# A gated transformer block on one core: e4m3 rounding done on float32 words read as int32, decoded by ScalarE's copies

## What is computed

```python
def _fp8(x):
    return x.astype(jnp.float8_e4m3fn).astype(jnp.float32)

def _reorder_quantize_x(x, idx):
    scale = jnp.max(jnp.abs(x)) / GLOBAL_DIV
    xr = (x / scale)[:, idx]
    scale_x = jnp.max(jnp.abs(xr), axis=1, keepdims=True) / FP8_MAX
    qx = _fp8(xr / scale_x)
    return (qx, scale_x, scale)
...
qx, sx, sc = _reorder_quantize_x(xf, up_reorder_index)
g = _qlinear(qx, sx, sc, w_gate, up_reorder_index, out_idx=down_reorder_index)
u = _qlinear(qx, sx, sc, w_up, up_reorder_index, out_idx=down_reorder_index)
t = jax.nn.silu(g) * u
qt, st, sct = _reorder_quantize_x(t, down_reorder_index)
y = _qlinear(qt, st, sct, w_down, down_reorder_index)
...
x = x + tanh(g_xattn[0]) * xattn(layernorm(x), ctx_512, Wq, Wkv_expand, Wout)
x = x + tanh(g_ffn[0]) * ffn(layernorm(x), w_gate, w_up, w_down, up_reorder_index, down_reorder_index)
```

## Time and profile before

| | |
|---|---|
| time, median of 3 runs | 765.31 us (764.86 to 766.76) |
| span of the profiled execution, first to last instruction | 761.7 us |
| between the span and the median of the runs | 3.6 us |
| busy share: PE, DVE, ACT, POOL | 87%, 92%, 73%, 74% |
| mean granted TensorE clock | 0.967 |

### The profile page before, as it was taken

One profiled execution on the slowest core, in us unless ns is written; L12 is line 12 of the kernel. 1 busy time (PEld: TensorE's weight loads), 2 busy tenths in 40 slices (PEclk: granted clock), 3 DMA queues, 4 the chain that ended last, 5 costly groups with the idle time before them and its releaser, 6 DMA issues.

```text
span 761.7 us, 15793 instructions
## 1 busy us (share of the span) xinstructions
PE 665.4 (87%) x6054; PEld 416.8 (55%) x6130; DVE 701.5 (92%) x1177; ACT 553.4 (73%) x987; POOL 563.7 (74%) x606
## 2 busy tenths in 40 slices
PE   2466888999999999999999999999999999787672
PEld 2455665656565665666665656565656565443220
DVE  6998696999999999999999999999999999997983
ACT  4978888887869696878787878788787857374330
POOL 5588897877878787878787878788787876565351
PEclk9878999999999999999999999999999999999986
DMA  9789775696575657574756584946465655041221
GB/s 290 191 201 187 158 148 102 125 190 122 139 115 133 120 130 133 128 126 107 145 115 131 98 164 83 174 83 167 83 162 102 142 87 124 8 103 26 62 65 46
DMA packets 151209, 95.52 MB, mean 125 GB/s; under 512 B 115327, under 2 KB 121855, under 8 KB 151135
## 3 DMA queue, kind: packets, MB, share of 16 engines
q1 hardware_dynamic: 148974, 92.68, 57.6%
q0 software_dynamic: 576, 1.45, 0.6%
q10 hardware_dynamic: 1584, 0.39, 0.3%
HBM read 31.59 MB, written 9.83 MB: 54 GB/s over the span
## 4 chain that ended last, share of the span: by engine, by line
DVE 54%; ACT 15%; issue 12%; PE 10%; POOL 5%; DMA 2%; ACTq 0%; SPq 0%; DVEq 0%; POOLq 0%; another core or an unknown queue 0%
DVE mx L1687 8%; DVE room L1773 7%; DVE room L1554 6%; DVE mx L1686 5%; PE pair L726 4%; DVE tm L1780 3%; DVE rsum L1691 3%; DVE cx L1735 3%; DVE room L1798 3%; DVE room L1756 3%; ACT PT L1334 2%; DVE room L1558 2%; POOL x L607 2%; POOL PT L587 2%; ACT L1334 2%
## 5 line engine op out<-in xcount | busy, mean ns | idle before, releaser
L603 POOL TENSOR_TENSOR room<-room,up_scale 128x512 f32<-128x512 f32 (+1 forms) x96 | 132.6, 1388 | 42.9 <-ACT room L1359 40.4
L587 POOL TENSOR_SCALAR_AFFINE_SELECT PT<-PT 128x512 f32<-128x512 f32 x128 | 84.5, 678 | 40.5 <-ACT PT L1334 40.2
L1359 ACT ACTIVATE room<-room,sx 128x512 f32<-128x512 f32 (+1 forms) x96 | 65.2, 681 | 57.9 <-DVE room L1756 57.2
L1334 ACT ACTIVATE PT<-pair 128x768 f32<-128x768 f32 x128 | 98.9, 817 | 8.0 <-PE pair L958 7.0
L726 PE MATMUL pair<-WdT,room 128*128 128x512 bf16 x349 | 84.6, 391 | 18.4 <-DMA room<-room 12.8
L726 PE MATMUL pair<-WgT,room 128*128 128x512 bf16 (+1 forms) x370 | 88.4, 361 | 8.1 <-DMA room<-room 4.3
L726 PE MATMUL pair<-WuT,room 128*128 128x512 bf16 (+1 forms) x369 | 89.0, 363 | 2.5 <-DVE room L1756 1.9
L726 PE MATMUL pair<-xT,WqTh 128*128 128x256 bf16 x512 | 87.1, 273 | 1.7 <-ACT exact L1146 1.7
L1364 ACT ACTIVATE room<-room 128x512 bf16<-128x512 f32 (+1 forms) x96 | 54.7, 586 | 45.3 <-DVE room L1773 44.3
L1687 DVE TENSOR_REDUCE mx<-pair 128x2 f32<-128x512 f32 x128 | 86.9, 679 | 0.0
L726 PE MATMUL pair<-xT,WqTl 128*128 128x256 bf16 x256 | 69.8, 272 | 0.0
(11 more groups left out here) (137 smaller groups left out, 1948.7 us busy)
## 6 DMA issues: line engine op xcount, KB each, us to landing
xin<-in_x_dram SPq DMA_DIRECT2D x16, 512.0 KB
K<-kh SPq DMA_DIRECT2D x32, 256.0 KB
Q<-qh SPq DMA_DIRECT2D x32, 256.0 KB
x<-in_x_dram SPq DMA_DIRECT2D x16, 512.0 KB, 4.3
out_dram<-x SPq DMA_DIRECT2D x16, 512.0 KB, 3.1
K<-kl SPq DMA_DIRECT2D x16, 256.0 KB
Q<-kl SPq DMA_DIRECT2D x16, 256.0 KB
room<-in_L_ffn_w_down_dram SPq DMA_DIRECT2D x4, 704.0 KB, 7.4
```

The lines of the kernel that those rows point to most:

```text
L587: pool.affine_select(out=view, in_=view, compare_op=ALU.is_ge, fill=0.0, base=0, pattern=[[0, 2], [0, 2], [1, P]], channel_multiplier=-1). ...
L603: pool.tensor_tensor(g, g, up_scale[:, chunk(n)[1]], ALU.mult).then_inc(slw_done, 1)
L1334: act.activation(head_columns(ring(b, c), 0, 384), head_columns(shifted_pair[c][:, :], 0, 384), ACT.Exp, scale=SCALE).then_inc(exp_done, 1)
L1359: act.activation(g, g, ACT.Silu, scale=sx[:, chunk(n)[0]:chunk(n)[0] + 1]).then_inc(silu_done, 1)
```

## The change

The rounding is done on float32 words. With x * mult * 2^-120 the smallest normal number of e4m3 falls on the smallest normal number of float32, and its step below falls among float32's subnormals. The word, read as int32, is turned to float by VectorE, which adds 1.5 * 2^43 and subtracts it again: that rounds it to a multiple of 2^20, which leaves three fraction bits. The result is written back over the same word. Its upper half is a bfloat16, and a copy by ScalarE with the factor 2^120 decodes it.

- VectorE does `scaled` (factor per row, then 2^-120) and `coded` (on int32) in place of `floored`, `lifted` and `low`: two instructions for a tile and not three, with one input each and 32-bit words in and out.
- ScalarE's absolute values are gone. For x and t a copy takes their place behind `coded` (`taken_x`, `taken_t`), each of a whole tile; for the weights TensorE transposes the upper halves, and the copy that ScalarE made before gets the factor.
- GpSimd no longer rounds weights.
- `q_w` is gone; its room gives six raw slots. Unit u waits for the transposes of unit u - 6 (before: for the rounding of unit u - 4).
- `squares2` of token tile 1 moves ahead of `exps` 6 (`coded` overwrites `cx`), and waits are added for the buffers that are now shared longer.

```diff
-ROUND_FLOOR = 1.5 * 2.0**-6
-ROUND_LIFT = 2.0**20
+CODE = 2.0**-120
+ROUND = 1.5 * 2.0**43
...
-    SLOTS = 4
+    SLOTS = 6
...
+        def code_tile(u, n):
+
+            return raw_tile(u, n).bitcast(BF16).rearrange("p (n two) -> p n two", two=2)[:, :, 1]
...
             def unit_loaded(u):
...
+                if u >= SLOTS:
+                    sp.wait_ge(w_turned, u - SLOTS + 1)
...
             def turn_qt(b, t):
+                if b:
+                    sp.wait_ge(down_made, 2 * b - 1 + t)
                 sp.wait_ge(qt_done, 2 * b + t + 1)
...
-            def abs_t(b, n):
-                act.wait_ge(t_done, 6 * b + n + 1)
-                t, f = chunk(n)
-                act.activation(qt[:, t, f], T[:, t, f], ACT.Abs, scale=ROUND_LIFT).then_inc(abst_done, 1)
+            def taken_t(b, t):
+                act.wait_ge(codedt_done, 2 * b + t + 1)
+                if b:
+                    act.wait_ge(qtT_in[t], 16 * b)
+                act.activation(qt[:, t, :], T[:, t, :], ACT.Copy, scale=1.0 / CODE).then_inc(qt_done, 1)
...
-            def low(dst, w, high):
-                return dve.tensor_tensor(dst, w, high, ALU.subtract)
-
-            def floored(lift, mult):
-
-                return dve.tensor_scalar(lift, lift, mult, ROUND_FLOOR * ROUND_LIFT, ALU.mult, ALU.max)
+            def scaled(w, mult):
+
+                return dve.tensor_scalar(w, w, mult, CODE, ALU.mult, ALU.mult)
+
+            def coded(w):
+
+                return dve.tensor_scalar(w.bitcast(I32), w.bitcast(I32), ROUND, -ROUND, ALU.add, ALU.add)
...
-            def lifted_t(b, t):
-                dve.wait_ge(floort_done, 2 * b + t + 1)
-                dve.scalar_tensor_tensor(out=T[:, t, :], in0=T[:, t, :], scalar=tmult[:, t:t + 1], in1=qt[:, t, :],
-                                         op0=ALU.mult, op1=ALU.add).then_inc(liftedt_done, 1)
-
-            def rounded_t(b, t):
-                dve.wait_ge(liftedt_done, 2 * b + t + 1)
-                low(qt[:, t, :], T[:, t, :], qt[:, t, :]).then_inc(qt_done, 1)
+                scaled(T[:, t, :], tmult[:, t:t + 1]).then_inc(scaledt_done, 1)
+
+            def coded_t(b, t):
+                dve.wait_ge(scaledt_done, 2 * b + t + 1)
+                coded(T[:, t, :]).then_inc(codedt_done, 1)
```

More of the change, by code:

```diff
@@ L15 @@
 BF16 = mybir.dt.bfloat16
+I32 = mybir.dt.int32
 ALU = mybir.AluOpType
@@ L142, in gated_block_kernel @@
         SLOT = max(2 * H, I)
-        room = sb("room", [P, SLOTS * SLOT + SLOTS * SLOT // 2])
+        room = sb("room", [P, SLOTS * SLOT])
         carved = [0]
@@ L228, in raw_tile, with all_tiles @@
             return raw_w[:, u % SLOTS, n * width:(n + 1) * width]
[L230 to L234, removed]
+        def code_tile(u, n):
+            return raw_tile(u, n).bitcast(BF16).rearrange("p (n two) -> p n two", two=2)[:, :, 1]
+        def all_tiles(u):
             j, _, k = UNITS[u]
-            return w[:, u % SLOTS, 0:k * (H if j < 2 else I)]
+            return raw_w[:, u % SLOTS, 0:k * (H if j < 2 else I)]
         def place(head):
@@ L786, in unit_turned @@
                     for m in range(k):
-                        last = pe.transpose(w[:, (i * k + m) * P:(i * k + m + 1) * P], q_tile(u, m)[:, tok(i)], identb[:, :])
+                        last = pe.transpose(w[:, (i * k + m) * P:(i * k + m + 1) * P], code_tile(u, m)[:, tok(i)], identb[:, :])
                 last.then_inc(w_turned, 1)
@@ L998, in gate_products @@
                     pe.wait_ge(qxT_in[1], 16 * b + 16)
+                if n == 3 and b >= 14:
+                    pe.wait_ge(y_done, 2 * b - 1)
                 if n == 3 and b < 14:
@@ L1376, in _ @@
             act.wait_ge(factor_done, 1)
-            for k in range(-8, NB + 1):
+            for k in range(-8, NB + 2):
                 at(k + 3, squares1, 0)
@@ L1678, in unit_rounded, with unit_coded @@
-            def unit_rounded(u):
-                dve.wait_ge(w_lifted, u + 1)
-                low(all_tiles(q_w, u), all_tiles(raw_w, u), all_tiles(q_w, u)).then_inc(w_round_dve, 1)
+                    last = scaled(raw_tile(u, m), wmult[:, j, i + m:i + m + 1])
+                last.then_inc(w_scaled, 1)
+            def unit_coded(u):
+                dve.wait_ge(w_scaled, u + 1)
+                coded(all_tiles(u)).then_inc(w_coded, 1)
             def maxima(b, c):
@@ L1763, in up @@
                     dve.wait_ge(up_made, 6 * b + 3)
+                if n % 3 == 0 and b:
+                    dve.wait_ge(qt_done, 2 * b + n // 3 - 1)
                 if n == 3:
@@ L1934, in _ @@
                 if k == 0:
[L1935 removed]
+                    unit_scaled(14)
                 if k == -5:
[L1937 removed]
+                    unit_coded(2)
                 at(k - 1, gate, 4)
```

382 lines of the change are left out of this document (74 added, 308 removed).

## The result

The changed kernel takes **752.34 us** (median of 4 runs, 750.39 to 752.92) where the kernel before takes 765.25 us beside it (764.86 to 766.76): a ratio of 0.983, 95% interval 0.982 to 0.985. That is 13 us less, and 738 us were forecast, 27 less. A second measurement on another chip gave 749.91 us (748.90 to 754.21), ratio 0.981 (0.978 to 0.985). The first reciprocal came at 95.44 us, so one of the signs of being wrong that the prediction names ("if that reciprocal stays at 96") is met. The profiled execution has a span of 750.5 us and a time of 752.25 us.

What follows compares the result with a forecast made beforehand. DVE was fullest (38.73 us of each 39.90 us period), PE close behind (38.38). Gains of 10.8 (twelve periods), 1.3, 0.5, 0.9, 10 (head) and 4 (end) made 27.5 us: span 734.2, plus 3.6, time 738 us, range 721 to 754.

Steps and rivals of the forecast that it cites:

- if that reciprocal stays at 96: Sign of being wrong: the first reciprocal of softmax sums staying at 96 us, where near 86 us was forecast.
- The instructions (7.0 us a sequence): DVE's new rounding of x and t, waits for GpSimd included: 7.0 us a sequence where it spent 12.4.
- Up to 95.91 ... I take 10: Head, where weights are prepared: DVE and ACT lose work, shortening it by 10 us, between 4 and 18.
- Loads: ... I cost that at nothing: Unit loads with six slots: later ones wait for a transpose on PE, costed at nothing.
- The first periods (2.7): Three periods after the first reciprocal: gains of 1.3 (165.74 to 205.99), 0.5 and 0.9 us.
- The regular period (39.0): Each of twelve periods: 39.0 us, between 38.4 and 40.4, with PE waiting for transposed t before `down` of tile 1.
- as long as ACT reaches the exponentials early: ACT's copy of t's tile 0 between exponentials 3 and 4 (1.4 us): hidden on this condition, otherwise up to 1 us.
- PE takes all: Rival: transposes land in time, periods are PE's 38.4 us, 42.5 us gained, 723 us; chance 0.17.
- `mT` would come 1 us earlier: In each period, DVE's time saved ahead of the third gate brings `mT` 1 us earlier.
- Twelve times 0.9: Twelve periods between 205.99 and 684.81 us, each 0.9 us shorter: 10.8 us.
- The end (4): Last stretch, 684.81 to 761.70 us: 4 us gained, between 0.8 and 9.6.
- the periods don't move: Rival: late landings, late exponentials or slow int32 step; only head, end and first periods gain, 750 us; chance 0.19.

Runs made afterwards that it cites:

- the repeat: The changed kernel itself measured again, nothing edited, on another chip: 749.91 us, ratio 0.981; first reciprocal 93.69 us.
- experiment 7: Changed kernel with the second rounding step (`coded`) on each tile of t done twice: 759.97 us, ratio 0.994 to the kernel before.
- Experiments 2: Changed kernel with the weights' second rounding step (`coded`) done on one column of each unit only: 752.68 us, ratio 0.985 to the kernel before.
- experiment 3: Half the bytes in unit loads from unit 6 on: changed kernel 748.08 us, ratio 0.978; kernel before 763.74 us, ratio 0.9995.
- experiment 11: Changed kernel with only x and t rounded the new way, weights the old way in four slots: 755.39 us, ratio 0.987 to the kernel before.
- experiment 10: Changed kernel with the load of `w_down` issued earlier, ahead of `stack_queries`: 747.82 us, ratio 0.979 to the kernel before.
- experiment 9: Changed kernel with `mT`'s DMA issued by SyncE and not ScalarE: 749.10 us, ratio 0.980 to the kernel before.
- experiment 8: Changed kernel with ScalarE's copy of t's tile 1 moved ahead of taking and sending `mT`: 750.92 us, ratio 0.983 to the kernel before.

## Why the prediction was off, step by step

- **The instructions (7.0 us a sequence)**: held, 6.54. The int32 step runs at the rate that I took; its median on 1408 columns is 894 ns (0.88 forecast), on 512 it is 428 (0.42). DVE is busy 33.9 us in a regular period (33.4 forecast).
- **"Up to 95.91 ... I take 10"** is the step that failed: 0.5 us in the profile, 2.2 in the repeat, 3.3 at most (experiment 7). I added up the time that DVE and ACT lose and looked only for how much of it was on the chain, not for what would be on the chain without it. DVE and ACT had hidden a chain of stacks (keys to `kl`, to K, to `kl` again, to Q, to `mT`, to Q) that is paced by DMAs of 5 to 8.5 us each, and two of these cost TensorE and GpSimd some 3 us more than before (K's low part and `mT`), in traffic that had moved against them. Experiments 2 and 3 show it from both sides: 12 us less on DVE gives nothing, half the bytes give 3 to 4 us, and in the kernel before the same half gives nothing. What ACT's share of the loss was worth by itself, and what the traffic beside `mT` costs, no run shows. My own row with DMA share for the head had it, and I did not read it. Of my bounds, 4 to 18, the lower one was too high: it counted ACT's instructions on the chain as if nothing stood beside them.
- **"Loads: ... I cost that at nothing"** holds as far as it was tried: the early loads crowd the queue (experiment 3), but the kernel with the old four slots (11) is no faster. That run has the old rounding of the weights too, so it does not price the slots by themselves.
- **The first periods (2.7)**: -2.5. Three us of that go with the load of `w_down`, itself late by 1.4 us and in front of the transposed x (experiment 10 gives them back): the work around it moved, the load was issued 2.0 us later, and the transpose followed it by 3.3 us and not by 4.6. It was a transfer that I had not followed at all, since it isn't in the diff. In the second period (37.44 for 36.65) TensorE waits 0.43 and 0.56 us for the exponentials, which it did not before; they stand behind the new copy on ACT.
- **The regular period (39.0)**: 39.05, right, and for the wrong reason, so this hit is luck. I took it as TensorE's 38.4 plus a wait for the transposed t. There is no such wait. The 38.4 is a mean over twelve periods, the last of which has less work for TensorE (33.4 us of busy time before, where the others have 38.9); a regular one after has 38.70. The other 0.35 us are the wait for `PT`, behind the copy of t's tile 0: I had that copy hidden, "as long as ACT reaches the exponentials early", and it is not quite. With my rival "PE takes all" I had set the floor at 38.4; experiment 9 shows 39.05. No run moves the copy of tile 0, so whether the 0.35 us can be had back is open. That `mT` would come 1 us earlier held (19.4 us after the reciprocal and not 20.4), and the path through ACT's copy of tile 1 has 0.4 us of slack (experiment 7).
- **Twelve times 0.9**: 6.7 and not 10.8. The regular ones give 0.8 each (39.87 to 39.06). Three us are lost to two landings of 5.0 us in place of 3.1, half a us to the last. The spread of 3.1 to 5.1 stood in the earlier trace rows; I took the median for all, and with 0.4 us of slack a late landing costs all but these 0.4. The rows mix both tiles: tile 1's alone landed in 4.3 us in most periods, beside `mT`'s DMA, and my reason for the 3.1, that this DMA is no longer on its way then, held.
- **The end (4)**: 6.6, and 5.0 in the repeat: under-sized by 1 to 3 us, and well under the upper bound of 9.6.
- The 3.6 us around the span are 1.8 when the profiled execution's own time is taken. The miss of 14.3 us is 9.5 + 5.2 + 4.1 - 2.6 less these 1.9, to rounding. That the time lies near my rival of 750 us, "the periods don't move", is chance: the regular periods moved by 0.8 us, and it was the head that did not.

## What to carry to other kernels

When work is taken off an engine, the gain ends at the next chain under it: take the engine away in thought and walk the chain again, DMAs and shared buffers included, before adding up what it saves. A DMA's landing isn't one number: with little slack nearly all of a late one is paid, so either give the path slack (here 1 us, from moving one DMA issue off the engine that also makes the data) or count the late ones; and look at what makes them late, since an earlier issue can also take the transfer out of its way. A mean over periods hides the one that is lighter: take the busy time of a regular period as the floor. And look at what the change pushes, by a few us, into the flight of a large transfer that it doesn't touch.

## What the runs showed of the hardware

The fetch of the program's instructions runs over the same DMA engines and shows in the trace as packets of 16 KB (0.9 to 2.2 us each) and 8 KB. The transpose of a tile of t lands in 3.1 us, and in 5.0 when such a packet falls into its end. Over the transposes of tile 1 in the 16 kernels with the new rounding of t, by where a 16 KB packet starts behind the transpose's issue:

| start of the packet behind the issue, us | landing, us |
|---|---|
| before the issue, or none in the flight | 3.1 (at most 3.3) |
| 0.6 to 0.8 | 3.7 to 4.0 (5.1 to 5.2 beside `mT`'s DMA) |
| 1.8 to 2.9 | 4.9 to 5.4 |
| 2.93 to 3.3 | 3.1 to 3.3 |

In experiment 8 and in the kernel before, where `mT`'s DMA runs beside the transpose, the first row is 4.3 to 4.7. The late landings are fixed by the place in the program: the same two sequences in nine profiles, two others after 34 matmuls were added on TensorE. One of the nine is experiment 11, in which DVE, ACT and GpSimd have other instructions and TensorE has the same matmuls, so these packets look like TensorE's own. The Trainium skill has a rule that fits (DMA: Bandwidth & Descriptors, Queues, rings and completion order): every DMA engine takes turns between the queues that have work, packet by packet, and a semaphore increment lands only after all earlier writes of that engine, across its queues. The trace agrees in that the transpose's last data packets are at 349.5 us and its last semaphore packets at 350.42, just when the 16 KB packet ends (349.41 + 1.01). It does not explain the whole delay: the landing is seen at 351.87, 1.45 us behind these packets, where in the regular period it is 0.5 us.
